# Adding the gate to the normed output on GpSimd, ahead of one output product, in the second retention layer

## The chip, the cores and the metric

One Trainium2 chip, one core. The metric is the device time of one execution in microseconds (us); lower is better. The kernel runs as one launch with one instruction stream for each engine: PE (TensorE, with its weight loads shown as PEld), DVE (VectorE), ACT (ScalarE), POOL (GpSimd) and SP (SyncE, which issues most loads). The engines run their own streams in order and meet only at semaphores.

## What is computed

A two-layer transformer on 16 sequences of 512 tokens, width 128: a retention with a gate, a mixture of eight experts (top two of each token), a second retention, a second mixture of experts, a layer norm behind each. The change lies in the second retention, which is this part of the reference (eight heads of 16):

```
scores = einsum('bnhd,bmhd->bhnm', q, k) * D
ret = einsum('bhnm,bmhd->bnhd', scores, v)
mu, var = mean(ret), var(ret)                     # over the 16 features of a head
ret = (ret - mu) * rsqrt(var + EPS)
ret = ret.reshape(B, S, HIDDEN) * gn_w + gn_b
gated = x @ W1
out = gated * sigmoid(gated) + ret
return out @ W2
```

The residual and the layer norm follow, and then a router: logits of the eight experts, the two largest of them, and the rank that each token gets in its expert's list.

## The kernel before, in words

The second retention is a pipeline over the 16 sequences, written out step by step by hand. In step s the engines work on seven sequences at once, each at another stage. The stages are named by the variables of `turns(s)`: `y` sums the expert results of layer one, `a` (two steps behind the load) makes q, k, v, `b` the scores and the retention itself, `c1` the norm of each head, `c2` the output product, `d` the router, `e` the scatter of rows to the experts. So the output product of a sequence stands one step behind its head norm. The order in each engine's stream is the order of these statements; there is no planner.

What the change touches, in the order of one step:

- PE, `step`: the gate product `x @ W1` (L2384, tile T1) of sequence b, right behind it the eight small matmuls that count the ranks of the router (`ranks_mm_`, L405 to L413) of the sequence that was at d one step earlier, then the scores (L2281). Further on `project_out(c2)`: two rank-one products that put in the constant row (L2312, L2315), and for each of four blocks of 128 tokens the gate's block times `w_2` (L2319) and the normed output's block times `w_2g` (L2321), all summed in the PSUM tile T0. In the profile each product is two instructions. Behind it: the first part of the retention product (L2298), a wait for the second half of the masked scores, the q and k products (L2449, L2450), the transposes of the head norm's factors (L2465).
- ACT: the gate's SiLU into `sgT` (L2021), and `oc`, a copy of the retention's raw output (L2063).
- DVE: `oT` (L2214), the normed output, is `oc` times the transposed factors. Right behind it stands the router's `choose`: copy of the logits, the two largest, their indices, `dif` (L390), a cast (L392), `pick` (L393), `picked` (L398). PE's rank matmuls wait for `picked`. DVE then waits for the ranks and makes the rows (`rows_of`, L421 to L431); behind these stand the masked scores of the first half (L2119), the states, the head norm's inverse root (L209 to L216), the masked scores of the second half, the sums of the expert results (L1640, L1654), the residual `r` (L2129), q and k (L2205, L2206), and `oT` again.
- POOL: four pairs of scatters of sequence e (L477), two small power operations (L295, L297) for the norms of y and c2, then `put_places` of d (a mark at L189, copies at L453 and L456), which waits for a tanh on ACT (L444).
- Set-up on ACT, at the end of layer one: `w_2`, and `w_2g`, which is `w_2` with its rows scaled by `gn_w` (L1093).
- `HELD` (17) is the number of buffers in which layer one's expert results wait for their scatter on POOL (L897); ACT's copy into a buffer (L969) waits until the scatter that last read it has landed.

Of the kernel before, what the change touches and what calls it, by code (L numbers as in the profile page):

```python
# [15 lines left out]
P = 128  # L16
SEQS, T, D = 16, 512, 128
# [87 lines left out]
def build(nc, x, x_T, w_proj, wo, gnorm, rope, router0, gate0, up0, down0,  # L105
# [9 lines left out]
    with whole:  # L115
# [38 lines left out]


        sent_sems = [[whole.enter_context(nc.semaphore(f"sent{l}{i}")) for i in range(2)] for l in range(2)]
        HELD = 17
        st_sems = [[whole.enter_context(nc.semaphore(f"st{l}{i}")) for i in range((HELD, 4)[l])] for l in range(2)]
        used = []

# [460 lines left out]
        def first_layer(block):  # L621
            ph = ExitStack()
            with ph:
# [292 lines left out]
                def _(act):  # L916
# [142 lines left out]
                    for u in range(STEPS + DRAIN):  # L1059
                        unit(u)  # L1060
                        if u == 2:
                            late_rows(t14)
                        if u == 3:
                            late_turned_rows(t14)
                        if u == 4:
                            act.wait_ge(ogT_mm, SEQS)
                            nc.scalar.copy(ogT[:], TT).then_inc(ogT_ev, 1)
                            turned_logits(t14, O)
                            late_copies(t14)
                        if u == 7:  # L1070
                            late_rows(t15)
                        if u == 8:
                            late_turned_rows(t15)
                            late_copies(t15)
                        if u == 9:
                            turned_logits(t15, O)
                        if u == ALONE + 20:
                            exp_piece()
                        if u == ALONE + 24:
                            tanh_piece()  # L1080
                        if u == EARLY_STEPS + 18:
                            comb.norm.squares(act, comb.r[0], first_two[0], comb.used)
                        if u == EARLY_STEPS + 20:
                            comb.norm.squares(act, comb.r[1], first_two[1], comb.used)
                        if u == EARLY_STEPS + 21:
                            comb.norm.apply(act, comb.r[0], xb[0], first_two[0], x2_there)
                        if u == FOLD:
                            act.wait_ge(s_early, 16 * len(early))
                            act.wait_ge(wv_mm, 1)
                            nc.scalar.copy(w_v[:], V_BANK[:, 0:P]).then_inc(wv_there, 1)  # L1090
                            act.wait_ge(w2_mm, 1)
                            nc.scalar.copy(w_2[:], W_BANK[:, 0:P]).then_inc(w2_there, 1)
                            nc.scalar.activation(w_2g[:], W_BANK[:, 0:P], ACT.Copy, scale=g_w[:, 0:1]).then_inc(w2_there, 1)  # L1093
                            comb.norm.apply(act, comb.r[1], xb[1], first_two[1], x2_there)
                        if u == FOLD + 1:
                            act.wait_ge(gb_mm, 1)
                            nc.scalar.copy(gb_hi[:], G_BANK[0:1, 0:D]).then_inc(gb_hi_there, 1)
# [230 lines left out]
                def _(pe):  # L1328
# [215 lines left out]
                    for u in range(STEPS + DRAIN):  # L1544
# [42 lines left out]
                            nc.tensor.matmul(V_BANK[:, 0:P], w_vT[:], c_center[:], start=True, stop=True).then_inc(wv_mm, 1)  # L1587
                            nc.tensor.matmul(W_BANK[:, 0:P], w_2T[:], c_mean[:], start=True, stop=True).then_inc(w2_mm, 1)
                        if u == FOLD + 1:
                            pe.wait_ge(w2_there, 2)  # L1590
                            nc.tensor.matmul(G_BANK[0:1, 0:D], g_b[:], w_2[:], start=True, stop=True).then_inc(gb_mm, 1)

            return Ends(e_y_mm, e_y_there, wv_there, w2_there, set_there)
# [71 lines left out]
        def second_layer(block, first):  # L1665
# [4 lines left out]
            with ph:  # L1670
# [71 lines left out]
                g_mm, sg_there = sem("g_mm"), sem("sg_there")  # L1742
                o_mm, sq_there, oc_there = sem("o_mm"), sem("sq_there"), sem("oc_there")
                var_mm, var_there, ex_mm, oT_there = sem("var_mm"), sem("var_there"), sem("ex_mm"), sem("oT_there")
                yb_there = sem("yb_there")
                y_mm, r_there, x3_there, x3_kept = sem("y_mm"), sem("r_there"), sem("x3_there"), sem("x3_kept")

# [111 lines left out]
                def _(pool):  # L1859
                    norm.set_up(pool)  # L1860

                    def unit(u):
                        n = u - 5
                        if 0 <= n < STEPS:
                            pool.wait_ge(e_idx_there, n + 1)
                            pool.wait_ge(e_y_there, n + 1)
                            for i in range(ROWS // P):
# [2 lines left out]
                                        ap=idx[n % 4][:, i:i + 1], axis=0),  # L1870
                                    in_=ysb[n % 4][:, i, :], in_offset=None).then_inc(e_st[n % 4], 16)

                    def paced(y, a, b, c1, c2, d, e):
                        if e:
                            router.scatter_pair(pool, e, 0)
                            if d:
                                router.scatter_pair(pool, e, 1, router.tp, d.n + 1)
                                router.scatter_pair(pool, e, 2, router.lg_mm, d.n + 1)
                            else:
                                router.scatter_pair(pool, e, 1)  # L1880
                                router.scatter_pair(pool, e, 2)
                            if b:
                                router.scatter_pair(pool, e, 3, sT_there, 4 * b.n + 4)
                            else:
                                router.scatter_pair(pool, e, 3)
                        if y and y.n > 2:
                            comb.norm.power(pool, y)
                        if c2:
                            norm.power(pool, c2)

                    def step(s, fill):
                        _, y, a, b, c1, c2, d, e = turns(s, lags + [7])
# [3 lines left out]
                        else:  # L1896
# [3 lines left out]
                            for q in range(4):  # L1900
                                if e:
                                    router.scatter_pair(pool, e, q)
                            fill(2)
                            fill(3)
                        if d:
# [29 lines left out]
                def _(act):  # L1935
# [58 lines left out]
                    def step(s, fill):  # L1994
# [60 lines left out]
                        if b:  # L2055
# [4 lines left out]
                            wait_count(act, var_mm, b.n)  # L2060
                            nc.scalar.activation(osq[:], O[:, :], ACT.Square).then_inc(sq_there, 1)
                            wait_count(act, oT_there, b.n)
                            nc.scalar.copy(oc[:], O[:, :]).then_inc(oc_there, 1)  # L2063
                        else:
                            fill(3)
                        if d:
# [201 lines left out]
                def _(pe):  # L2268
# [1 line left out]
                    pe.wait_ge(s_cleared, 1)  # L2270
                    pe.wait_ge(first.y_there, STEPS)
                    pe.wait_ge(first.wv_there, 1)
                    pe.wait_ge(first.w2_there, 2)
                    pe.wait_ge(first.set_there, 2)

                    def scores(b, half):
# [30 lines left out]
                                             start=False, stop=False, skip_group_check=True)  # L2307

                    def project_out(c2):
                        pe.wait_ge(oT_there, c2.n + 1)  # L2310
                        pe.wait_ge(sg_there, c2.n + 1)
                        nc.tensor.matmul(T0[:].rearrange("p (c d) -> p c d", c=CH), ones_r[:],  # L2312
                                         gb_hi[:].unsqueeze(1).to_broadcast([1, CH, D]), start=True, stop=False,
                                         skip_group_check=True)
# [1 line left out]
                                         gb_lo[:].unsqueeze(1).to_broadcast([1, CH, D]), start=False, stop=False,  # L2316
                                         skip_group_check=True)
                        for i in range(CH):
                            nc.tensor.matmul(T0[:, i * D:(i + 1) * D], sgT[c2.odd][:, i * P:(i + 1) * P], w_2[:],  # L2319
                                             start=False, stop=False, skip_group_check=True)  # L2320
                            mm = nc.tensor.matmul(T0[:, i * D:(i + 1) * D], oT[:, i * P:(i + 1) * P], w_2g[:],  # L2321
                                                  start=False, stop=True, skip_group_check=True)
                        mm.then_inc(y_mm, 1)

# [170 lines left out]
        with weights:  # L2495
# [12 lines left out]
            def shared_sem(name):  # L2508
                return weights.enter_context(nc.semaphore("b_" + name))

            w_v, w_2, w_2g = (shared_sb(n, [P, P]) for n in ("wv", "w2", "w2g"))
            gb_hi, gb_lo = shared_sb("gb_hi", [1, D], F32R), shared_sb("gb_lo", [1, D], F32R)
            ones_r = shared_sb("ones_r", [1, P], F32R)
            xb = [shared_sb(f"xb{i}", [P, CH, D]) for i in range(2)]
# [93 lines left out]
```

## Time and profile before

| | us |
|---|---|
| median of 3 runs | 1215.84 |
| runs, lowest to highest | 1214.67 to 1220.07 |
| the profiled execution, its own time | 1216.78 |
| span of that execution | 1214.9 |
| second retention, first to last output product in the trace | 570 to 824 |

| engine | busy us | share of the span |
|---|---|---|
| PE | 1119.5 | 92% |
| PEld | 999.6 | 82% |
| DVE | 905.6 | 75% |
| ACT | 742.2 | 61% |
| POOL | 730.4 | 60% |

The shares are means over stages with different limits, and PE's busy time includes matmuls that overlap each other. So the rows further down come from the second retention alone: which engine there waits for which, in the order of time. Two times on DVE can overlap a little, because an instruction is drawn until its last write while the next one has begun.

### The profile page before, as it was taken

To read this page: it belongs to the slowest core of one execution; us is meant where nothing else is said; L and a number is where in the kernel's file an instruction comes from. 1 tells how busy PE (TensorE), PEld (TensorE's weight loads), DVE (VectorE), ACT (ScalarE), POOL (GpSimd) and SP (SyncE) were. 2 spreads that over 40 slices of the span, in tenths; PEclk is the share of its full clock that TensorE was granted. 3 is DMA by queue.
4 is the path that set the end of the run, shared out by engine and by line. 5 is a ranking of instruction groups with operands and counts; after the bars stand their busy time and mean duration, and the time that the engine had idled before them with its cause. 6 is when DMAs were issued, how large, how long until landed. Compare 5 with 4: busy or idle time off the path is not lost.

```text
span 1214.9 us, 31631 instructions
## 1 busy us (share of the span) xinstructions
PE 1119.5 (92%) x10400; PEld 999.6 (82%) x10400; DVE 905.6 (75%) x2648; ACT 742.2 (61%) x2015; POOL 730.4 (60%) x901
## 2 busy tenths in 40 slices
PE   8999999998788999978999999966999999999991
PEld 5888888886678999956777777655899999999991
DVE  4688988998666777747888988865676666667873
ACT  2345435554455777744777888744566666667884
POOL 0257777776467777473366766566744444445765
PEclk9999999999899999989999999977999999999996
DMA  8212111211124433352332211111321121214553
GB/s 235 79 60 73 38 53 48 73 32 55 51 76 128 129 109 108 117 160 69 97 117 67 71 51 49 45 36 45 102 58 55 56 58 56 57 56 123 154 180 123
DMA packets 75423, 101.77 MB, mean 84 GB/s; under 512 B 15138, under 2 KB 51490, under 8 KB 74850
## 3 DMA queue, kind: packets, MB, share of 16 engines
q1 hardware_dynamic: 49538, 59.89, 17.6%
q0 software_dynamic: 17280, 35.69, 8.8%
q10 hardware_dynamic: 8448, 4.20, 1.2%
q8 instruction: 87, 1.43, 0.5%
q14 instruction: 70, 0.57, 0.2%
HBM read 59.87 MB, written 43.04 MB: 85 GB/s over the span
## 4 chain that ended last, share of the span: by engine, by line
PE 69%; DVE 17%; ACT 5%; issue 4%; POOL 2%; SPq 1%; DMA 1%; ACTq 1%; DVEq 0%; POOLq 0%
PE banks L2353 16%; PE banks L2372 10%; PE banks L1444 6%; PE banks L1462 4%; DVE a_sT L1116 3%; PE banks L1353 2%; PE banks L2298 2%; PE banks L1383 2%; PE banks L2290 2%; PE banks L2449 2%; PE banks L2281 2%; ACT a_r_x L260 2%; PE banks L2319 1%; PE banks L1380 1%; DVE a_qm L1218 1%
## 5 line engine op out<-in xcount | busy, mean ns | idle before, releaser
L1868 POOL DMA_INDIRECT expert_out<-e_ysb,b_e_idx x142 | 161.5, 1137 | 149.3 <-ACT e_ysb L1973 122.5
L2353 PE MATMUL banks<-b_e_x_hi,e_w_hi 128*128 128x256 f32 x568 | 166.4, 293 | 4.5 <-ACT e_sgl L1963 2.4
L897 POOL DMA_INDIRECT expert_out<-a_e_ysb,a_e_idx x142 | 140.8, 991 | 44.4 <-issue 36.2
L2353 PE MATMUL banks<-b_e_x_hi,e_w_lo 128*128 128x256 f32 x568 | 159.7, 281 | 0.0
L477 POOL DMA_INDIRECT scattered<-a_r_x,a_r_idx x128 | 127.6, 997 | 33.9 <-issue 33.9
L2372 PE MATMUL banks<-w_dn,e_h 128*128 x1136 | 138.3, 275 | 2.3 <-DVE e_h L2165 1.6
L2372 PEld LDWEIGHTS banks<-w_dn,e_h 128*128 128x128 f32 x1136 | 132.5, 192 | 3.0 <-issue 2.9
L2165 DVE TENSOR_TENSOR e_h<-banks,e_sgl 128x512 f32<-128x512 f32 x142 | 97.1, 689 | 49.5 <-PE banks L2353 47.0
L1963 ACT ACTIVATE e_sgl<-banks 128x512 f32<-128x512 f32 x142 | 85.1, 599 | 74.8 <-DVE e_h L2165 41.8
L477 POOL DMA_INDIRECT scattered<-b_r_x,b_r_idx x112 | 110.0, 982 | 30.9 <-issue 30.9
L2153 DVE TENSOR_TENSOR e_w_lo<-w_gu,e_w_hi 128x1024 fp32r<-128x1024 f32 x71 | 87.0, 1226 | 54.7 <-ACT e_w_hi L1952 54.7
L2353 PEld LDWEIGHTS banks<-b_e_x_hi,e_w_hi 128*128 128x128 f32 x568 | 107.5, 189 | 6.1 <-ACT e_sgl L1963 3.3
L2353 PEld LDWEIGHTS banks<-b_e_x_hi,e_w_lo 128*128 128x128 f32 x568 | 107.2, 189 | 0.0
L2353 PE MATMUL banks<-e_x_lo,e_w_hi 128*128 128x256 f32 x376 | 105.6, 281 | 0.0
L1444 PE MATMUL banks<-a_e_x_hi,a_e_w_hi 128*128 128x256 f32 x284 | 88.4, 311 | 0.2 <-DVE a_e_h L1167 0.2
L2119 DVE TENSOR_TENSOR b_sT<-banks,c_causal 128x1024 f32<-128x1024 f32 x64 | 75.4, 1219 | 15.6 <-PE banks L2281 15.1
L1462 PE MATMUL banks<-w_dn,a_e_h 128*128 x568 | 76.5, 277 | 10.3 <-ACT a_e_ysb L969 10.3
L1952 ACT CAST e_w_hi<-w_gu 128x1024 fp32r x71 | 74.2, 1045 | 13.7 <-PE banks L2353 5.2
L1444 PE MATMUL banks<-a_e_x_hi,a_e_w_lo 128*128 128x256 f32 x284 | 81.9, 288 | 0.0
L1444 PE MATMUL banks<-a_e_x_lo,a_e_w_hi 128*128 128x256 f32 x284 | 81.3, 286 | 0.0
L1462 PEld LDWEIGHTS banks<-w_dn,a_e_h 128*128 128x128 f32 x568 | 69.5, 191 | 13.2 <-issue 13.1
L863 POOL TENSOR_TENSOR a_inv_rms<-a_mse,c_half 128x16 f32<-128x16 f32 x14 | 47.6, 3402 | 45.1 <-DVE a_mse L1133 45.1
(385 smaller groups left out, 3292.1 us busy)
## 6 DMA issues: line engine op xcount, KB each, us to landing
a_e_xg<-scattered SPq DMA_DIRECT2D x71, 130.0 KB
b_e_xg<-scattered SPq DMA_DIRECT2D x71, 130.0 KB, 2.0
b_cy<-expert_out SPq DMA_DIRECT2D x32, 256.0 KB, 3.2
f_y<-expert_out SPq DMA_DIRECT2D x32, 256.0 KB, 3.5
a_xT<-in_x_T SPq DMA_DIRECT2D x16, 256.0 KB, 2.8
out<-f_x ACTq DMA_DIRECT2D x16, 256.0 KB, 2.9
expert_out<-a_e_ysb,a_e_idx POOLq DMA_INDIRECT x142, 2.3
expert_out<-e_ysb,b_e_idx POOLq DMA_INDIRECT x142
```

The costliest lines, as they stand in the source:

```text
L477: nc.gpsimd.indirect_dma_start(out=scattered[0:E * REGION, :], out_offset=bass.IndirectOffsetOnAxis(ap=self.rows_at(t)[:, j:j + 1], axis=0 ...
L897: nc.gpsimd.indirect_dma_start(out=expert_out, out_offset=bass.IndirectOffsetOnAxis(ap=idx[n % HELD][:, i:i + 1], axis=0), in_=ysb[n % HEL ...
L1444: mm = nc.tensor.matmul(bank_of(c)[:, i * ROWS:(i + 1) * ROWS], w_[c % RING][:, g, f:f + P], x_[c % RING][:], start=(k == 0), stop=(k == 2))
L1462: mm = nc.tensor.matmul(y_bank(d)[:, i * D:(i + 1) * D], h[d % RING][:, f, i * P:(i + 1) * P], w_dn[:, bass.ds(e, 1), f, :].rearrange("p o ...
L1868: nc.gpsimd.indirect_dma_start(out=expert_out, out_offset=bass.IndirectOffsetOnAxis(ap=idx[n % 4][:, i:i + 1], axis=0), in_=ysb[n % 4][:, ...
L1952: nc.scalar.copy(w_hi[b % RING][:], w_gu[:, bass.ds(e, 1), :, :].rearrange("p o g f -> p (o g) f")).then_inc(e_w_hi_there, 1)
L1963: nc.scalar.activation(sgl[j][:], gate_bank(c, j)[:].rearrange("p (k n) -> p k n", k=2), ACT.Silu).then_inc(e_sg_there, 1)
L2119: nc.vector.tensor_tensor(sT[half][:, 2 * g:2 * g + 2, :, :].rearrange("p g n t -> p (g n) t"), pairs[2 + g].rearrange("p g (n t) -> p (g ...
L2153: nc.vector.tensor_tensor(w_lo[b % RING][:], w_gu[:, bass.ds(e, 1), :, :].rearrange("p o g f -> p (o g) f"), w_hi[b % RING][:].bitcast(F32 ...
L2165: nc.vector.tensor_tensor(h[c % RING][:, 2 * j:2 * j + 2, :], up_bank(c, j)[:].rearrange("p (k n) -> p k n", k=2), sgl[j][:], ALU.mult).th ...
L2353: mm = nc.tensor.matmul(bank_of(c, j)[:, i * ROWS:(i + 1) * ROWS], w_[c % RING][:, g, f:f + P], x_[c % RING][:], start=(m == 0), stop=(m = ...
L2372: mm = nc.tensor.matmul(y_bank(d)[:, i * D:(i + 1) * D], h[d % RING][:, f, i * P:(i + 1) * P], w_dn[:, bass.ds(e, 1), f, :].rearrange("p o ...
```

## The change

The gate and the normed output are added before the output product, so that `w_2` is applied once and not twice. For that the norm's weight `gn_w` moves from `w_2g` into ACT's copy `oc`, which becomes an activation with a scale for each partition; `w_2g` and the ACT instruction that made it are gone. The sum is one POOL instruction, `oT = oT + sgT` (128 by 512, f32), with its own semaphore `osum_there`; PE's `project_out` waits for that one in place of `oT_there` and `sg_there`. For that semaphore one of layer one's result buffers is given up (`HELD` 17 to 16). The rank matmuls keep their place behind the gate product.

```
-        HELD = 17
+        HELD = 16
...
-                            nc.scalar.activation(w_2g[:], W_BANK[:, 0:P], ACT.Copy, scale=g_w[:, 0:1]).then_inc(w2_there, 1)
...
+                    def gated_sum(c1):
+                        pool.wait_ge(oT_there, c1.n + 1)
+                        pool.wait_ge(sg_there, c1.n + 1)
+                        nc.gpsimd.tensor_tensor(oT[:], oT[:], sgT[c1.odd][:], ALU.add).then_inc(osum_there, 1)
...
                         if c2:
                             norm.power(pool, c2)
+                        if c1:
+                            gated_sum(c1)
...
                             for q in range(4):
                                 if e:
                                     router.scatter_pair(pool, e, q)
+                            if c1:
+                                gated_sum(c1)
...
-                            nc.scalar.copy(oc[:], O[:, :]).then_inc(oc_there, 1)
+                            nc.scalar.activation(oc[:], O[:, :], ACT.Copy, scale=g_w[:, 0:1]).then_inc(oc_there, 1)
...
                     def project_out(c2):
-                        pe.wait_ge(oT_there, c2.n + 1)
-                        pe.wait_ge(sg_there, c2.n + 1)
+                        pe.wait_ge(osum_there, c2.n + 1)
...
                         for i in range(CH):
-                            nc.tensor.matmul(T0[:, i * D:(i + 1) * D], sgT[c2.odd][:, i * P:(i + 1) * P], w_2[:],
-                                             start=False, stop=False, skip_group_check=True)
-                            mm = nc.tensor.matmul(T0[:, i * D:(i + 1) * D], oT[:, i * P:(i + 1) * P], w_2g[:],
+                            mm = nc.tensor.matmul(T0[:, i * D:(i + 1) * D], oT[:, i * P:(i + 1) * P], w_2[:],
                                                   start=False, stop=True, skip_group_check=True)
```

POOL in one step of the full pipeline, before: the last pair of scatters, the two power operations of the norms, and the places.

```order
L477 DMA scattered<-b_r_x,b_r_idx 67584x130 x2
L295 TENSOR_TENSOR b_cn_ve<-b_cn_var,b_cn_eps 128x4
L297 TENSOR_TENSOR b_cn_rstd<-b_cn_ve,c_half 128x4
L295 TENSOR_TENSOR b_n_ve<-b_n_var,b_n_eps 128x4
L297 TENSOR_TENSOR b_n_rstd<-b_n_ve,c_half 128x4
L189 TENSOR_TENSOR mark<-c_half 1x1
L453 COPY b_r_x<-c_place 128x4
```

The same piece of POOL's stream after the change:

```order
L477 DMA scattered<-b_r_x,b_r_idx 67584x130 x2
L295 TENSOR_TENSOR b_cn_ve<-b_cn_var,b_cn_eps 128x4
L297 TENSOR_TENSOR b_cn_rstd<-b_cn_ve,c_half 128x4
L295 TENSOR_TENSOR b_n_ve<-b_n_var,b_n_eps 128x4
L297 TENSOR_TENSOR b_n_rstd<-b_n_ve,c_half 128x4
L1876 TENSOR_TENSOR b_oT<-b_oT,b_sgT 128x512
L189 TENSOR_TENSOR mark<-c_half 1x1
L453 COPY b_r_x<-c_place 128x4
```

One instruction came in, between the last power operation and the places of the same step.

POOL in the last but two steps of the pipeline (s = 19), after the change, where the step has another order: the norm's power operations, the scatters of a sequence in one go, and the sum behind them.

```order
L295 TENSOR_TENSOR b_n_ve<-b_n_var,b_n_eps 128x4
L297 TENSOR_TENSOR b_n_rstd<-b_n_ve,c_half 128x4
L189 TENSOR_TENSOR mark<-c_half 1x1
L477 DMA scattered<-b_r_x,b_r_idx 67584x130 x8
L1876 TENSOR_TENSOR b_oT<-b_oT,b_sgT 128x512
```

Here the last sequence's sum stands behind eight scatters; before, no instruction of POOL stood between the last sequence's `oT` and its output product.

PE in one step, from the router's logits to the q and k products, before (the pair L2319, L2321 stands there four times):

```order
L364 MATMUL banks<-b_wr,b_r_xT 128x8 x4
L2312 MATMUL banks<-b_gb_hi,b_ones_r 128x512
L2315 MATMUL banks<-b_gb_lo,b_ones_r 128x512
L2319 MATMUL banks<-b_w,b_sgT 128x128
L2321 MATMUL banks<-b_w2g,b_oT 128x128
...
L2298 MATMUL banks<-b_sT,b_vz 32x128 x8
L2449 MATMUL banks<-b_xT,b_wq 128x512
```

And after (the lines have moved by six to nine):

```order
L364 MATMUL banks<-b_wr,b_r_xT 128x8 x4
L2320 MATMUL banks<-b_gb_hi,b_ones_r 128x512
L2323 MATMUL banks<-b_gb_lo,b_ones_r 128x512
L2327 MATMUL banks<-b_w,b_oT 128x128 x4
L2307 MATMUL banks<-b_sT,b_vz 32x128 x8
L2455 MATMUL banks<-b_xT,b_wq 128x512
```

Four of the eight products are gone from each of the 16 output products; nothing else in PE's stream moved.

## Rows read from the trace of the kernel before

**Rows 1.** Busy us by engine in a stretch; columns: PE, PEld, DVE, ACT, POOL, PEclk, DMA.

```profile
570.00:760.00 190.00, 188.06 (x2043) 145.30 (x2043) 168.08 (x598) 145.25 (x497) 118.43 (x212) 1.00 0.24 73
```

**Rows 2.** Waits in 560 to 800: us in total, times, longest.

```profile
DVE b_r_rows L421 <- PE banks L413: 9.0, 12, 0.8
```

**Rows 3.** Timeline of DVE in one step: start us, us, operation [idle before].

```profile
689.90 2.35 DVE L2119 TENSOR_TENSOR b_sT<-banks,c_causal 128x1024 f32<-128x1024 f32 x2
...
695.12 0.68 DVE L2205 TENSOR_TENSOR b_qr<-banks,b_tq 128x512 f32<-128x512 f32 x1
695.72 0.68 DVE L2206 TENSOR_TENSOR b_kT<-banks,b_tk 128x512 f32<-128x512 f32 x1
696.49 0.69 DVE L2214 TENSOR_TENSOR b_oT<-banks,b_oc 128x512 f32<-128x512 f32 x1
...
698.69 0.23 DVE L393 TENSOR_TENSOR b_r_pick<-c_iota,b_r_ix 128x64 f32<-128x64 f32 x1
698.95 0.19 DVE L398 TENSOR_TENSOR b_r_picked<-b_r_pick 128x32 bf16<-128x32 f32 x1
...
699.91 0.19 DVE L421 TENSOR_TENSOR b_r_rows<-banks,base 128x32 f32<-128x32 f32 x1 [0.77 <-PE banks L413]
```

**Rows 4.** Timeline of PE in the same step, to the next step's q product.

```profile
692.63 1.12 PE L2449 MATMUL banks<-b_xT,b_wq 128*128 128x512 f32 x2
...
699.53 0.18 PE L405 MATMUL banks<-b_r_picked,c_tri 128*128 128x32 bf16 x1
...
707.67 0.39 PE L2319 MATMUL banks<-b_w,b_sgT 128*128 128x128 f32 x2
707.90 0.39 PE L2321 MATMUL banks<-b_w2g,b_oT 128*128 128x128 f32 x2
...
709.68 1.12 PE L2449 MATMUL banks<-b_xT,b_wq 128*128 128x512 f32 x2
```

**Rows 5.** Timeline of POOL in the same step.

```profile
697.45 1.01 POOL L297 TENSOR_TENSOR b_n_rstd<-b_n_ve,c_half 128x4 f32<-128x4 f32 x1
700.57 0.18 POOL L189 TENSOR_TENSOR mark<-c_half 1x1 f32<-1x1 f32 x1 [2.11 <-ACT b_r_th L444]
```

**Rows 6.** Timeline of DVE and PE at the ranks of step 17.

```profile
786.93 0.19 DVE L398 TENSOR_TENSOR b_r_picked<-b_r_pick 128x32 bf16<-128x32 f32 x1
...
787.17 0.19 PE L405 MATMUL banks<-b_r_picked,c_tri 128*128 128x32 bf16 x1 [0.83 <-DVE b_r_picked L398]
...
787.57 0.19 DVE L421 TENSOR_TENSOR b_r_rows<-banks,base 128x32 f32<-128x32 f32 x1 [0.45 <-PE banks L413]
```

**Rows 7.** Timeline of PE and POOL at the last sequence's output product.

```profile
819.53 0.79 PE L2312 MATMUL banks<-b_gb_hi,b_ones_r 1*128 1x512 f32 x1
...
820.81 0.96 POOL L477 DMA_INDIRECT scattered<-b_r_x,b_r_idx  x1 [0.30 <-issue]
```

**Rows 8.** Busy us by engine there; columns as in rows 1.

```profile
820.00:824.00 4.00, 4.00 (x17) 3.35 (x17) 0.61 (x5) 0.00 (x0) 2.23 (x7) 0.50 0.10 33
```

**Rows 9.** Timeline of DVE and POOL, two places where both read SBUF.

```profile
706.22 0.24 DVE L214 TENSOR_TENSOR b_gn_sq<-b_gn_y 128x32 f32<-128x32 f32 x1
706.24 0.96 POOL L477 DMA_INDIRECT scattered<-b_r_x,b_r_idx  x1 [0.30 <-issue]
...
810.40 1.23 DVE L2153 TENSOR_TENSOR e_w_lo<-w_gu,e_w_hi 128x1024 fp32r<-128x1024 f32 x1 [1.92 <-ACT e_w_hi L1952]
810.66 1.01 POOL L189 TENSOR_TENSOR mark<-c_half 1x1 f32<-1x1 f32 x1
```

**Rows 10.** POOL's groups by line: busy us, mean ns of one.

```profile
L841 POOL MEMSET c_half<- 128x64 f32 x1 | 0.2, 151 | 0.3 <-POOLq L2598 0.3
L844 POOL MEMSET a_wr<- 128x24 f32 x1 | 0.1, 118 | 0.0
```

**Rows 11.** Timeline of ACT at the set-up of the second retention.

```profile
520.74 0.37 ACT L1093 ACTIVATE b_w2g<-banks,b_gw 128x128 f32<-128x128 f32 x1
521.00 1.27 ACT L303 ACTIVATE b_xb<-b_cr,b_cn_rstd 128x128 f32<-128x128 f32 x4
```

More of the change, by code:

```diff
@@ L1589, in _ @@
                         if u == FOLD + 1:
-                            pe.wait_ge(w2_there, 2)
+                            pe.wait_ge(w2_there, 1)
                             nc.tensor.matmul(G_BANK[0:1, 0:D], g_b[:], w_2[:], start=True, stop=True).then_inc(gb_mm, 1)
@@ L1744, in second_layer @@
                 var_mm, var_there, ex_mm, oT_there = sem("var_mm"), sem("var_there"), sem("ex_mm"), sem("oT_there")
+                osum_there = sem("osum_there")
                 yb_there = sem("yb_there")
@@ L2272, in _ @@
                     pe.wait_ge(first.wv_there, 1)
-                    pe.wait_ge(first.w2_there, 2)
+                    pe.wait_ge(first.w2_there, 1)
                     pe.wait_ge(first.set_there, 2)
@@ L2509, in shared_sem @@
                 return weights.enter_context(nc.semaphore("b_" + name))
-            w_v, w_2, w_2g = (shared_sb(n, [P, P]) for n in ("wv", "w2", "w2g"))
+            w_v, w_2 = (shared_sb(n, [P, P]) for n in ("wv", "w2"))
             gb_hi, gb_lo = shared_sb("gb_hi", [1, D], F32R), shared_sb("gb_lo", [1, D], F32R)
```

## The prediction

> **What bounds the kernel now.** The mean shares say PE (92%), so I read the stage that is changed by itself: first busy time by stage, then the waits, then one step on three engines in the order of time. In the full pipeline PE is busy 188 of 190 us at its full 2.4 GHz level (granted clock 1.00), but DVE is busy 168 of them too [rows 1], and the small gaps between dependent DVE instructions come on top. A step takes 17.05 us (709.68 less 692.63) [rows 4]. Of DVE's idle time one wait stands out: 12 times, 9.0 us in all, it waits for the router's ranks [rows 2]. One step shows why [rows 3, 4]. `picked` ends at 699.14 (698.95 + 0.19). The rank matmul starts at 699.53, 0.39 later, with no idle time shown before it: PE was still in the gate product that stands ahead of it. DVE goes on at 699.91. In step 17, where PE had nothing else to do, `picked` ends at 787.12, the matmul starts 0.05 later, and DVE goes on 0.45 after `picked` [rows 6], not 0.77. So PE and DVE are both nearly full and hold each other at the ranks. A shorter PE stream alone is worth what DVE can follow, no more.
>
> **The change part by part.**
>
> Four products fewer. Products follow each other 0.23 us apart (707.67, 707.90) [rows 4]; the eight take some 1.8 us, so four save 0.9 us in each step, 14 us of PE in 16. What lies behind them decides what is kept. The q product L2449 may start only when DVE has ended the second half of the masked scores: 689.90 + 2.35 = 692.25, and it started at 692.63 [rows 3, 4]. With the reaction time of 0.05 to 0.06 [rows 6] it can start at 692.31, so PE keeps 0.32 of the 0.9; the rest becomes a wait for the mask. The gate product and the ranks follow 0.32 earlier, at 699.21. DVE can deliver: `oT` stood 0.77 behind `kT`, while `kT` stood 0.60 behind `qr` [rows 3]; I read the 0.17 as a wait for PE's transposes, which goes, and `picked` then ends at 698.97, ahead of 699.21. So without any other effect a full step gets 0.32 us shorter.
>
> The sum on POOL. No row shows such an instruction. Two fills on POOL give a slope: 33 ns for 40 elements [rows 10], 0.8 ns an element, about 0.1 us to begin with. The write alone, 512 elements, is 0.5 us; two reads in turn and a write beside them 0.95; all three in turn 1.4. I take 1.2 us, between the last two, and keep 0.5 and 1.4 as ends. In place it costs POOL nothing: the power operation ahead of it ends at 698.46, and the mark behind it starts at 700.57, after 2.11 us of idle time [rows 5]. `oT` is there at 697.18, so the sum runs from 698.46 to about 699.66. The places are not late until it takes more than 2.1 us, and PE's output product comes some 8 us later in the next step.
>
> What it costs is DVE. Just then DVE has `pick` and `picked` to do, each with both inputs in SBUF, and PE's ranks wait for them. Two rows show that POOL and DVE do not read freely side by side [rows 9]. POOL's mark, one element, lasts 1.01 us where a mark takes 0.18 [rows 5]: it ends at 811.67, when DVE's subtraction of two SBUF tiles (810.40 to 811.63) ends. POOL is held for all of DVE's instruction. The other way round the trace has only short cases: a DVE product of two SBUF inputs takes 0.24 where the same line elsewhere takes 0.19, as POOL's scatter starts 0.02 behind it and fetches its indices. So the hold on DVE lies between 0.05 us and the whole sum. I take the whole: the full hold is what the long case shows, and the sum, unlike the scatter, reads from its beginning to its end. `pick` would start at 698.52 (698.69 less 0.17) and has to wait until 699.66; from its start to the end of `picked` it is 0.45 (698.69 to 699.14), so 700.11; 0.45 more for the ranks gives 700.56, where DVE now goes on at 699.91. That is 0.65 us more in a step: the hold of 1.14 less the waits of 0.49 that the shorter PE stream has opened. By the ends of the sum (0.95 and 1.4) it is 0.40 and 0.85.
>
> The Trainium skill has a rule for this (SBUF — State Buffer, Who interferes with whom): a DVE instruction with two SBUF inputs and a GpSimd instruction that reads SBUF share one read interface, whichever starts first has it for the whole instruction, and the other "fully blocks". The first case of rows 9 agrees (1.01 us); no run here shows the reverse at length. By that rule a step is 0.65 longer, by the short row alone (0.05) it is 0.27 shorter. The same skill (GPSIMD Engine Reference, Performance versus the Vector engine) gives 4497 ns for an add of 2048 columns; a quarter, as an estimate, is 1.1 us, and a step would then be 0.55 longer; no row here shows it.
>
> How many steps. The wait for ranks stands in 12 steps, 6 to 17 [rows 2]; I charge each 0.65: 7.8 us. In the four steps ahead of them no ranks are counted, and the sum meets no DVE work that matters: nothing.
>
> The last two output products. There the step has another order and the clock is at the 1.2 GHz level (0.50) [rows 8], so four products are worth 1.8 us (twice 0.9). The last but one gives that, and pulls forward all behind it, POOL's eight scatters too. The last one loses it again: its sum stands behind these scatters, which end at 821.77 (820.81 + 0.96), 2.24 later than PE starts now [rows 7]. With 1.8 earlier scatters: 819.97 + 1.2 = 821.2, that is 1.6 late, against 1.8 saved by its own four products. Net I take 0; between 1 gained and 1 lost.
>
> The small parts. `w_2g` frees 0.26 us of ACT (521.00 less 520.74) [rows 11], back to back with what starts the second retention: 0.26 gained, between 0 and that. `oc` with a scale instead of a copy is the same kind of ACT instruction with the same tile, off the path: 0. One buffer fewer (`HELD`): the trace lists no wait of ACT for a free buffer; a wait would cost a pair of scatters, 2 x 1.26 us as in rows 7 (0.96 + 0.30), once or twice. I take 0.
>
> Sum: 7.8 - 0.26 + 0 = 7.5 us. The profiled execution took 1216.78, so 1224.3; it lies 0.94 above the median of the runs, so the median comes to 1215.84 + 7.5 = 1223.3.
>
> **The rivals.**
>
> *DVE is not held, or hardly.* Then the shorter PE stream counts: 12 x 0.32 = 3.8, 0.26 from ACT, and 0 to 1 at the end, together 4.6: 1211.2 (with all ends 1209.5 to 1212). For it: the only rows with DVE second show 0.05 us; against it: the full hold on POOL. It decides at a hold of 0.49 us in a step: below, the change gains.
>
> *The sum takes far longer than the fills suggest*, 2 us, because its reads wait for DVE's in between. Then a step is 1.45 longer, 12 x 1.45 = 17.4: 1233. For it: POOL waited 0.8 us for one DVE instruction [rows 9]; against it: behind `pick` and `picked` DVE has only short ones.
>
> *The clock falls.* PE would idle about 2 us in each step of 17.7; if the granted clock then fell to its 1.2 GHz level now and then, as it is in rows 8 after long waits, the 16 us of PE work would outgrow the step: one such stretch of 4 us costs up to 2 us of PE, hidden by the idle time at first. Several in each step would give over 1235. Against it: the idle time is cut into pieces of 1 us.
>
> *The change does not do what it says*: the four products are gone in the order of instructions, so only the price of each could be wrong; that is in the first rival.
>
> **How the numbers follow.** DVE held for about the sum: 0.64, own range 1219.5 (0.40 a step, and 1 gained at the end) to 1227 (0.85, and 1 lost). Not held: 0.25. A far longer sum: 0.08. Clock: 0.03. Faster by over 0.5% (about what a measurement of this kernel can tell from no change; 6.1 us, so below 1209.8) needs the first rival at its end: 0.07. Slower by over 0.5% (above 1221.9) is most of the held case, 0.45, and the last two: 0.56. The rest, 0.37, is within. The range reaches down to the first rival and up past the held case: 1210 to 1228.
>
> **What would show it.** In the profile after: a POOL instruction of 128x512 right behind `b_n_rstd`, about 1.2 us; `pick` on DVE starting at its end, where it now follows the cast at once; PE idle before the rank matmul, about 1 us, for `picked`; steps of 17.7 us. If `pick` starts on time and steps are 16.7 us, the hold was wrong. If steps are longer but `pick` is on time, look for what else is late. In the last step, the output product should start right behind the sum, not behind the ranks.

## The result, and the profile after

The changed kernel takes 1224.82 us in the median of 9 runs (1222.37 to 1227.9), the kernel before 1215.84: ratio 1.0068, 95% interval 1.0056 to 1.0080. It is slower by about 9 us; the forecast was 1223.3. The profiled execution of after took 1222.74 (span 1220.9), that of before 1216.78, so the two traces account for 6.0 us; the other 3 lie between executions that were not traced, and stay open. One execution of before_sum (2664.55) and one of held16 (2716.24) took more than twice as long as the others, and the medians further down leave them out.

Three rows of one full step carry the result. First POOL, in the order of time (start us, us, operation, idle before):

```profile
698.13 1.01 POOL L297 TENSOR_TENSOR b_n_rstd<-b_n_ve,c_half 128x4 f32<-128x4 f32 x1
699.11 1.26 POOL L1876 TENSOR_TENSOR b_oT<-b_oT,b_sgT 128x512 f32<-128x512 f32 x1
701.01 0.18 POOL L189 TENSOR_TENSOR mark<-c_half 1x1 f32<-1x1 f32 x1 [0.64 <-ACT b_r_th L444]
```

The sum takes 1.26 us and stands where POOL was idle: the mark still waits 0.64 for ACT, where it waited 2.11 [rows 5]. Now DVE in the same step:

```profile
697.00 0.68 DVE L2223 TENSOR_TENSOR b_oT<-banks,b_oc 128x512 f32<-128x512 f32 x1
...
698.91 0.17 DVE L390 TENSOR_TENSOR b_r_dif<-b_r_mx 128x4 f32<-128x4 f32 x1
...
699.20 1.25 DVE L393 TENSOR_TENSOR b_r_pick<-c_iota,b_r_ix 128x64 f32<-128x64 f32 x1
700.49 0.19 DVE L398 TENSOR_TENSOR b_r_picked<-b_r_pick 128x32 bf16<-128x32 f32 x1
...
701.13 0.19 DVE L421 TENSOR_TENSOR b_r_rows<-banks,base 128x32 f32<-128x32 f32 x1 [0.45 <-PE banks L413]
```

`pick` lasts 1.25 us where it lasted 0.23 [rows 3]. It is not shown as waiting: it is drawn from 699.20 on and ends (700.45) just behind the sum (700.37). The ranks are then 0.45 away, as in step 17 of before [rows 6], not 0.77. And PE:

```profile
692.99 1.12 PE L2455 MATMUL banks<-b_xT,b_wq 128*128 128x512 f32 x2 [0.31 <-DVE b_sT L2128]
...
699.02 1.02 PE L2390 MATMUL banks<-b_xT,b_w 128*128 128x512 f32 x2
700.74 0.19 PE L405 MATMUL banks<-b_r_picked,c_tri 128*128 128x32 bf16 x1 [0.69 <-DVE b_r_picked L398]
...
710.30 1.12 PE L2455 MATMUL banks<-b_xT,b_wq 128*128 128x512 f32 x2 [0.25 <-DVE b_sT L2128]
```

PE now waits twice in a step for DVE: 0.69 for `picked`, and 0.25 to 0.31 for the masked scores. The step is 17.31 us (710.30 less 692.99), where it was 17.05 [rows 4]. Over 190 us PE is busy 177.73, DVE 173.13, and the granted clock stays at 1.00, the 2.4 GHz level; the row of before is in [rows 1]:

```profile
570.00:760.00 190.00, 177.73 (x1933) 132.04 (x1931) 173.13 (x593) 142.70 (x488) 132.01 (x221) 1.00 0.23 72
```

### The profile page after: what moved, and what is told of

Its sections match the earlier page's. It is cut to its first block, busy times and chain, and to the rows that moved or that the text cites. A ratio compares the mean times of both kernels' runs of the same rounds, so it can differ in the third digit from the quotient of the medians.

```text
span 1220.9 us, 31402 instructions
## 1 busy us (share of the span) xinstructions
PE 1111.4 (91%) x10272; PEld 987.3 (81%) x10272; DVE 915.7 (75%) x2648; ACT 741.8 (61%) x2014; POOL 749.2 (61%) x917
## 3 DMA queue, kind: packets, MB, share of 16 engines
q8 instruction: 86, 1.41, 0.5%
## 4 chain that ended last, share of the span: by engine, by line
PE 57%; DVE 26%; issue 6%; ACT 5%; POOL 3%; SPq 1%; DMA 1%; ACTq 1%; DVEq 0%; POOLq 0%
PE banks L2359 16%; PE banks L2378 10%; PE banks L1443 6%; PE banks L1461 4%; DVE a_sT L1115 3%; DVE b_sT L2128 3%; PE banks L1382 2%; PE banks L1352 2%; PE banks L2299 2%; ACT a_r_x L260 1%; PE banks L1379 1%; DVE a_qm L1217 1%; PE banks L356 1%; DVE b_r_pick L393 1%; PE banks L2343 1%
```

## Where the time went, for all kernels

Four stretches add up to the span of a profile. Head: to the q product of step 6 (590.36 in before). Eleven steps: from there to the q product of step 17. Drain: to the start of the last residual `r`. Rest: the second mixture of experts and the end. The step in brackets is the mean of the eleven; in no_sum and late_last, for instance, one step that is longer than the others lifts it by up to 0.1. The lower rows are the experiments that follow; each ratio there is to runs of the kernel before taken beside it (medians 1215.56 to 1216.14).

| kernel | median us | head | eleven steps (one) | drain | rest |
|---|---|---|---|---|---|
| before | 1215.84 | 590.36 | 187.49 (17.04) | 46.65 | 390.40 |
| after | 1224.82 | 588.84 | 190.68 (17.33) | 49.71 | 391.67 |
| no_sum | 1208.62 | 588.47 | 182.04 (16.55) | 45.10 | 390.79 |
| before_sum | 1230.15 | 590.78 | 194.13 (17.65) | 52.97 | 390.72 |
| sum_early | 1212.45 | 589.64 | 181.85 (16.53) | 48.94 | 390.67 |
| sum_halves | 1224.14 | 591.32 | 189.21 (17.20) | 50.64 | 391.43 |
| last_dve | 1221.21 | 589.93 | 190.51 (17.32) | 46.71 | 391.45 |
| early_last | 1211.54 | 591.38 | 182.16 (16.56) | 45.99 | 390.67 |
| sum_late | 1215.51 | 589.19 | 181.14 (16.47) | 48.90 | 391.37 |
| sum_dve | 1217.66 | 591.12 | 187.57 (17.05) | 47.61 | 391.30 |
| late_last | 1209.77 | 589.72 | 182.20 (16.56) | 44.58 | 390.50 |
| held16 | 1216.85 | 591.27 | 187.51 (17.05) | 46.58 | 390.24 |

Between before and after the stretches differ by -1.52, +3.19, +3.06 and +1.27, together +6.0. The head varies by 2.9 us among kernels that hardly differ there, so its -1.52 is no gain that can be claimed; the rest varies by 1.4, so neither is its +1.27 a loss. The eleven steps and the drain are where the change acts, and each loses about 3 us.

The drain of after, PE, POOL and DVE in the order of time:

```profile
788.35 0.97 DVE L390 TENSOR_TENSOR b_r_dif<-b_r_mx 128x4 f32<-128x4 f32 x1
...
805.17 1.19 DVE L390 TENSOR_TENSOR b_r_dif<-b_r_mx 128x4 f32<-128x4 f32 x1
...
807.27 0.49 PE L2320 MATMUL banks<-b_gb_hi,b_ones_r 1*128 1x512 f32 x1
...
810.11 0.69 DVE L2138 TENSOR_TENSOR b_r<-banks,xres 128x512 f32<-128x512 f32 x1 [1.67 <-PE banks L2327]
...
823.61 0.96 POOL L477 DMA_INDIRECT scattered<-b_r_x,b_r_idx  x1 [0.30 <-issue]
824.59 1.27 POOL L1876 TENSOR_TENSOR b_oT<-b_oT,b_sgT 128x512 f32<-128x512 f32 x1
...
826.00 0.76 PE L2320 MATMUL banks<-b_gb_hi,b_ones_r 1*128 1x512 f32 x1 [3.62 <-POOL b_oT L1876]
...
829.23 0.69 DVE L2138 TENSOR_TENSOR b_r<-banks,xres 128x512 f32<-128x512 f32 x1 [5.75 <-PE banks L2327]
```

And of before, beside [rows 7]:

```profile
803.49 0.49 PE L2312 MATMUL banks<-b_gb_hi,b_ones_r 1*128 1x512 f32 x1
...
807.32 0.69 DVE L2129 TENSOR_TENSOR b_r<-banks,xres 128x512 f32<-128x512 f32 x1 [2.68 <-PE banks L2321]
...
824.50 0.69 DVE L2129 TENSOR_TENSOR b_r<-banks,xres 128x512 f32<-128x512 f32 x1 [3.81 <-PE banks L2321]
```

In the last two steps the held instruction is `dif` (0.97 and 1.19 for 0.17). The last but one product takes 2.84 us to its residual, 3.83 before. From that residual to the last product it is now 15.89, before 12.21: eight scatters and the sum stand ahead of it. The last product then takes 3.23, before 4.97. With 2.11 until the last but one product (27.75 for 25.64) that is 2.11 - 0.99 + 3.68 - 1.74 = 3.06.

## Experiments

The theory: the sum holds a DVE instruction with two SBUF inputs until it ends, and in the drain the last sum stands behind the scatters. All kernels start from the changed one unless the text says otherwise.

**no_sum**, the four products fewer alone; the gate is missing from the output.

```diff
-                        if c1:
-                            gated_sum(c1)
...
-                            if c1:
-                                gated_sum(c1)
...
-                        pe.wait_ge(osum_there, c2.n + 1)
+                        pe.wait_ge(oT_there, c2.n + 1)
+                        pe.wait_ge(sg_there, c2.n + 1)
```

> The changed kernel with the POOL sum taken out; PE's output product waits for the normed output and the gate directly and multiplies the normed output alone, four products, so the gate is missing from the output. It shows what the four products fewer are worth without the sum. Theory of the hold (the sum keeps DVE's pick waiting 1.03 us a step): pick is back at 0.22 us, the step falls from 17.33 to between 16.45 and 16.75, the last output product no longer waits behind the scatters, and the time is 1203 to 1210. Rival (DVE is the bound with or without the sum, so four products less on PE bring nothing): the step only goes back to the 17.05 of the kernel before, the time is 1213 to 1217.

Measured: 1208.62, ratio to before 0.9944 (0.9926 to 0.9962); the full steps are 16.50.

```profile
694.21 0.23 DVE L393 TENSOR_TENSOR b_r_pick<-c_iota,b_r_ix 128x64 f32<-128x64 f32 x1
...
695.27 0.19 DVE L421 TENSOR_TENSOR b_r_rows<-banks,base 128x32 f32<-128x32 f32 x1 [0.61 <-PE banks L413]
```

`pick` is back at 0.23. So four products fewer are worth 0.5 us in a step and 7 us in all, the last output products included; the rival falls. The wait for ranks is 0.61 here, not 0.45: without the hold PE's gate product is again the later of the two.

**before_sum**, the sum alone, beside the eight products.

```diff
+                        nc.gpsimd.tensor_tensor(scratch[:], oT[:], sgT[c1.odd][:], ALU.add).then_inc(osum_there, 1)
...
-                        pe.wait_ge(oT_there, c2.n + 1)
-                        pe.wait_ge(sg_there, c2.n + 1)
+                        pe.wait_ge(osum_there, c2.n + 1)
```

> The kernel before with its eight products, and the POOL sum beside them into a tile that nobody reads; the output product waits for it as in the changed kernel (one result buffer is given up for the semaphore). It shows the sum's price by itself. Theory of the hold: pick takes 1.25 us instead of 0.22, the rank matmuls start 0.69 later than before (1.03 less the 0.39 that PE was still busy, and 0.05 of reaction), the step is 17.45 to 17.75, and with the last product behind scatters and sum (3.5 later) the time is 1225 to 1231. Rival (the sum costs DVE nothing that the pipeline feels; the loss of the changed kernel is in its last steps alone): the step stays at 17.05, the time is 1217 to 1221.

Measured: 1230.15, ratio 1.0118 (1.0096 to 1.0141), step 17.65. Time and step lie in the band; the held instruction was another. One step, POOL and DVE:

```profile
702.20 1.26 POOL L1878 TENSOR_TENSOR b_scratch<-b_oT,b_sgT 128x512 f32<-128x512 f32 x1
...
702.43 1.06 DVE L390 TENSOR_TENSOR b_r_dif<-b_r_mx 128x4 f32<-128x4 f32 x1
703.41 0.16 DVE L392 CAST b_r_ix<-b_r_mi 128x8 f32<-128x8 uint32 x1
703.60 0.23 DVE L393 TENSOR_TENSOR b_r_pick<-c_iota,b_r_ix 128x64 f32<-128x64 f32 x1
```

Here the sum starts 0.23 us ahead of `dif`, and `dif`, four columns long, pays: it lasts until 703.49, the sum until 703.46. In these runs the first instruction with two SBUF inputs that comes behind the sum's start is the one that is held, however short it is. That the step came so near is in part luck: the hold of 0.89 less the 0.32 at the ranks gives 0.57 of the 0.60, but two more terms that nobody had forecast cancel (`oT` stands 1.02 behind `kT` for 0.77, and the two masked scores stand 5.71 apart for 5.93).

**sum_halves**, two POOL instructions of 256 columns.

```diff
-                        nc.gpsimd.tensor_tensor(oT[:], oT[:], sgT[c1.odd][:], ALU.add).then_inc(osum_there, 1)
+                        for h in range(2):
+                            op = nc.gpsimd.tensor_tensor(oT[:, 256 * h:256 * h + 256], oT[:, 256 * h:256 * h + 256],
+                                                         sgT[c1.odd][:, 256 * h:256 * h + 256], ALU.add)
+                        op.then_inc(osum_there, 1)
```

> The changed kernel with the sum as two POOL instructions of 256 columns each. Theory that one instruction has the read port until its end and then lets the other engine in: pick is held by the first half alone and takes 0.6 to 0.75 us, the step is 16.7 to 16.95, the time 1216 to 1220. Rival that POOL keeps it as long as it has work queued: pick takes 1.25 us or more, step and time stay (17.3, 1224).

Measured: 1224.14, ratio 1.0066 (1.0044 to 1.0088), step 17.20.

```profile
700.70 1.41 POOL L1877 TENSOR_TENSOR b_oT<-b_oT,b_sgT 128x256 f32<-128x256 f32 x2
700.78 0.72 DVE L393 TENSOR_TENSOR b_r_pick<-c_iota,b_r_ix 128x64 f32<-128x64 f32 x1
701.53 0.62 DVE L398 TENSOR_TENSOR b_r_picked<-b_r_pick 128x32 bf16<-128x32 f32 x1
```

`pick` takes 0.72, as the theory of one lock for each instruction says; but then the second half holds `picked` (0.62 for 0.19). What this expectation left out is that `picked` also reads two SBUF operands. Together the hold is 0.92 in place of 1.03, and step and time miss the band: they lie near the rival's 17.3 and 1224, though the 0.72 of `pick` is not the rival's 1.25. Here the split gave the time between the two halves to the next reader, which the second half then held.

**sum_early**, the sum ahead of the second power operation, beside DVE instructions with at most one SBUF input.

```diff
-                        if c2:
-                            norm.power(pool, c2)
                         if c1:
                             gated_sum(c1)
+                        if c2:
+                            norm.power(pool, c2)
```

> The changed kernel with the sum moved on POOL ahead of the second power operation, so that it runs while DVE copies the logits (from PSUM) and takes maxima and indices (one SBUF input each), and is over when pick comes. Theory that the sum holds only an instruction with two SBUF inputs: pick is back at 0.22 us, the maxima and indices keep their times, the step is 16.45 to 16.75, the time is 1207 to 1214 (the last product still stands behind the scatters). Rival that the sum holds every DVE instruction that reads SBUF: some of the maxima or the copy become about 1 us longer, the step stays at 17.3, the time at 1223 to 1226.

Measured: 1212.45, ratio 0.9968 (0.9951 to 0.9984), steps of 16.50.

```profile
693.82 0.17 DVE L378 MAX8 b_r_mx<-b_r_lg 128x8 f32<-128x8 f32 x1
...
693.87 1.27 POOL L1876 TENSOR_TENSOR b_oT<-b_oT,b_sgT 128x512 f32<-128x512 f32 x1
693.90 0.29 DVE L378 MAX8 b_r_mx<-b_r_lg 128x8 f32<-128x8 f32 x3
...
694.91 0.26 DVE L390 TENSOR_TENSOR b_r_dif<-b_r_mx 128x4 f32<-128x4 f32 x1
...
695.36 0.23 DVE L393 TENSOR_TENSOR b_r_pick<-c_iota,b_r_ix 128x64 f32<-128x64 f32 x1
695.38 1.09 POOL L297 TENSOR_TENSOR b_n_rstd<-b_n_ve,c_half 128x4 f32<-128x4 f32 x1
695.62 0.19 DVE L398 TENSOR_TENSOR b_r_picked<-b_r_pick 128x32 bf16<-128x32 f32 x1
```

The same sum, of the same length, costs the step nothing here (16.50, as in no_sum): the maxima keep their times, and only `dif`, which starts 0.23 us before the sum ends, lasts 0.09 longer. The rival that the sum holds any read of SBUF falls. By moving one statement the change becomes faster than the kernel before.

**sum_late**, the sum behind the places, beside the masked scores.

```diff
-                        if c1:
-                            gated_sum(c1)
...
                             router.put_places(pool, d)
+                        if c1 and (y or a or b):
+                            gated_sum(c1)
```

> The changed kernel with the sum moved on POOL behind the places of its step, so that it runs beside DVE's masked scores (one input in PSUM, one in SBUF); the scatters of the next step come 1.2 us later, into POOL's idle time ahead of the places. Theory that only an instruction with two SBUF inputs is held: the masked scores keep their 2.35 us, pick its 0.22, the step is 16.45 to 16.75 and the time 1209 to 1215. Rival that one SBUF input is enough if the instruction reads it all along: the masked scores take about 3.5 us, the step is 17.3, the time 1222 to 1226.

Measured: 1215.51, ratio 0.9996 (0.9986 to 1.0005); the profiled execution, at 1212.49, is the lowest of its ten runs.

```profile
696.37 2.36 DVE L2128 TENSOR_TENSOR b_sT<-banks,c_causal 128x1024 f32<-128x1024 f32 x2
...
696.78 1.27 POOL L1876 TENSOR_TENSOR b_oT<-b_oT,b_sgT 128x512 f32<-128x512 f32 x1
```

The masked scores, one input in PSUM and one in SBUF, keep their 2.36 us with the sum inside them, and the step is 16.47: the theory holds. The median lies 0.5 us above the band, and 3 us above the profiled run; what differs in the other runs was not traced and stays open.

**last_dve**, the last sequence's sum on DVE.

```diff
-                            if c1:
-                                gated_sum(c1)
...
+                            if not (y or a or b):
+                                dve.wait_ge(oT_there, c1.n + 1)
+                                dve.wait_ge(sg_there, c1.n + 1)
+                                nc.vector.tensor_tensor(oT[:], oT[:], sgT[c1.odd][:], ALU.add).then_inc(osum_there, 1)
```

> The changed kernel with the last sequence's sum on DVE, right behind its normed output, and the other 15 on POOL as before. It tests the last output product. In the changed kernel it starts at 826.00, behind eight scatters and the sum, 3.6 us after the ranks. Theory (this wait is on the path to the end): DVE's sum takes about 0.65 (estimate: half of the 1.23 of its 1024-column subtraction of two SBUF tiles), the ranks come that much later and the product right behind them at about 822.9, so the time falls by 3.1, to 1220 to 1223. Rival (the experts that follow wait for something else): the product is earlier, the time stays at 1224 to 1225.

Measured: 1221.21, ratio 1.0041 (1.0027 to 1.0056).

```profile
820.87 0.69 DVE L2225 TENSOR_TENSOR b_oT<-b_oT,b_sgT 128x512 f32<-128x512 f32 x1
...
823.89 0.79 PE L2322 MATMUL banks<-b_gb_hi,b_ones_r 1*128 1x512 f32 x1
```

The last product starts right behind the ranks, and the drain is 46.71, that of before (46.65), for 49.71. So the wait behind the scatters is worth 3.0 us and is on the path to the end.

**early_last**, both at once.

> Both at once: the sum ahead of the second power operation, and the last sequence's sum on DVE. If the hold and the last product are separate costs, the time is that of the early sum (1212.5) less 3.1: 1207.5 to 1211, below the kernel before. If the last product was hidden, it is 1211 to 1214.

Measured: 1211.54, ratio 0.9963 (0.9947 to 0.9978), half a microsecond above the band and inside that of its rival (1211 to 1214), so the median alone does not decide. In the traces the two gains add: 16.56 a step and a drain of 45.99 for 48.94. The median shows 0.9 of these 3 us: the runs spread over 5 us, and the profiled execution's head is 1.7 longer than that of sum_early.

**sum_dve**, all sums on DVE.

> The changed kernel with all 16 sums on DVE, right behind the normed output, and none on POOL. Theory (DVE is the bound of the step once PE has four products less): each sum adds its own 0.6 to 0.7 us to a step of 16.50, so the step is 17.1 to 17.2 and the time 1215 to 1220, less than the changed kernel's because nothing is held and the last product does not wait for scatters. Rival (DVE, busy 75% of the span, has room): the step stays at 16.5, the time at 1208 to 1211.

Measured: 1217.66, ratio 1.0011 (0.9999 to 1.0023), step 17.05.

```profile
698.12 0.69 DVE L2218 TENSOR_TENSOR b_oT<-b_oT,b_sgT 128x512 f32<-128x512 f32 x1
...
698.28 0.59 POOL L295 TENSOR_TENSOR b_n_ve<-b_n_var,b_n_eps 128x4 f32<-128x4 f32 x1
```

The step lies just under the band (17.1 to 17.2). The sum takes 0.69 on DVE, and a step grows by 0.5 over no_sum; the wait for the ranks, 0.45 here for 0.61 there, gives back 0.16. So DVE has no more room than that, though it is busy only 75% of the span. The second row is the hold in the other direction: POOL's operation of four columns takes 0.59 for 0.19, until DVE's sum ends. So the sum takes less of DVE's time when DVE makes it (0.69) than when POOL makes it beside `pick` and holds DVE (1.03).

**late_last**, the late place in full steps, the early one in the last full step, the last sum on DVE. What the expectation calls the second to the thirteenth q product is the stretch from the fourth (573.07 in sum_late) to the sixteenth (770.33).

> The sum behind the places while the pipeline is full, ahead of the second power operation in the last full step (where the late place made the output product wait 2.09 us for it), and on DVE for the last sequence. By the parts of the traces so far: 197.3 us from the second to the thirteenth q product as with the late sum, then 46.0 to the last residual as with the early sum and the last on DVE, which is 7.6 less than before (250.85): 1207 to 1210. Rival (the late sum's runs scattered from 1212.5 to 1218 because its later scatters cost something that its one profile does not show): 1212 to 1216.

Measured: 1209.77, ratio 0.9954 (0.9937 to 0.9971): the lowest median of a complete kernel here, though early_last's interval (0.9947 to 0.9978) overlaps. The mean step is 16.56 and the drain 44.58, the shortest of all. By the medians it is about 15 us faster than the changed kernel with the same work. The median speaks for the theory, but three of the 12 runs lie above 1212 (up to 1217.21): the spread of the runs that the rival pointed at is still there, and its cause stays open.

**held16**, the kernel before with one result buffer fewer.

> The kernel before with 16 result buffers in the first layer in place of 17 and nothing else. Theory that no copy ever waits for the seventeenth buffer: ratio 1.000, 1214.5 to 1217. Rival that a copy waits once or twice for a pair of scatters (2.5 us each): 1218 to 1221.

Measured: 1216.85, ratio 1.0007 (0.9995 to 1.0019). No cost shows; the interval leaves room for at most 2.3 us, less than one such wait.

## Why the prediction was right, and where its steps were off

The sum's length and its place: 1.2 us was taken, 1.26 measured. The two halves give 0.71 each (1.41 for two), so it goes by 2.2 ns a column and 0.15 to begin with, between two and three times the fills' 0.8 ns an element. The prediction had bounded it so (0.95 to 1.4) and picked 1.2 without a row that says where between: there it was lucky.

The hold: 1.14 was charged, 1.03 measured (1.25 less 0.22), and no_sum, sum_early and sum_late show that it is the cause: without the sum, or with it beside instructions with other operands, the step is 16.5. One sign came otherwise: `pick` does not start at the sum's end, it starts on time and lasts. The rule of the Trainium skill that the prediction set beside [rows 9] (SBUF — State Buffer, Who interferes with whom) agrees for the sum in both directions: DVE instructions with two SBUF inputs are held until it ends (1.06 for `dif`), POOL's are held by DVE's sum (0.59 for 0.19). Beside the sum, one SBUF input is not held (`MAX8` at 0.17, masked scores at 2.36); beside a scatter that is not so, as the next rows show.

The step: 0.65 longer was forecast, 0.26 to 0.29 came. The step of the sum that failed is "the hold less the waits of 0.49 that the shorter PE stream has opened". The 0.49 was there (0.32 at the ranks, 0.18 from `r` to `oT`: 1.80 for 1.98), but 0.27 more was: between the two masked scores 5.66 us now (702.23 to 707.89), 5.93 before. The place is the inverse root. Groups of DVE over all 16 sequences (busy us, mean ns), before:

```profile
L210 DVE TENSOR_SCALAR b_gn_bits<-b_var 128x32 int32<-128x32 int32 x16 | 4.6, 290 | 0.0
L209 DVE TENSOR_SCALAR b_gn_half<-b_var 128x32 f32<-128x32 f32 x16 | 4.5, 283 | 0.5
```

and after:

```profile
L209 DVE TENSOR_SCALAR b_gn_half<-b_var 128x32 f32<-128x32 f32 x16 | 3.2, 202 | 0.5
L210 DVE TENSOR_SCALAR b_gn_bits<-b_var 128x32 int32<-128x32 int32 x16 | 2.9, 180 | 0.0
```

Both read one SBUF input. In each of the eleven steps of before, L210 ends together with one of POOL's scatters, in seven of them L209 too. One such place of before, POOL and DVE:

```profile
703.63 0.96 POOL L477 DMA_INDIRECT scattered<-b_r_x,b_r_idx  x1 [0.30 <-issue]
...
704.13 0.43 DVE L209 TENSOR_SCALAR b_gn_half<-b_var 128x32 f32<-128x32 f32 x1
704.23 0.36 DVE L210 TENSOR_SCALAR b_gn_bits<-b_var 128x32 int32<-128x32 int32 x1
```

All three end at 704.56 to 704.59. After the change the two start just ahead of a scatter or at its very beginning, and mostly take 0.18 each. In no_sum they lie inside a scatter, but earlier in it, and are not held either:

```profile
633.09 0.96 POOL L477 DMA_INDIRECT scattered<-b_r_x,b_r_idx  x1 [0.30 <-issue]
...
633.47 0.18 DVE L209 TENSOR_SCALAR b_gn_half<-b_var 128x32 f32<-128x32 f32 x1
633.56 0.17 DVE L210 TENSOR_SCALAR b_gn_bits<-b_var 128x32 int32<-128x32 int32 x1
```

The traces of all twelve kernels agree: from 560 to 830 us, where one of these two starts up to 0.49 us into a scatter, it takes 0.17 to 0.21; where it starts 0.53 or more into it, it ends no earlier than 0.03 us before the scatter does (at 0.50 and 0.51 both occur). So the kernel before already lost 0.27 in each step, and the new phase of the scatters took that away: 1.03 - 0.32 - 0.18 - 0.27 = 0.26. Of the 0.27, 0.19 stands at these two (from `b_var` to the next instruction 0.52 us for 0.71) and 0.05 at the square at 706.22, where another scatter begins [rows 9]. No experiment moved the scatters alone, so that they are the cause rests on this agreement. The same missing term made the first rival too small: it allowed 0.32 a step for four products, no_sum shows 0.5. By these terms the change gains from a hold under 0.77, not 0.49; sum_halves fits, with a hold of 0.92 and a step 0.15 longer than before.

The drain: 0.65 was forecast (the last of the twelve charged steps, and net 0 for the products), +3.06 came. Two terms were off. The last but one product gave 0.99, not 1.8: TensorE's clock was not at the lower level from its start. In before it was granted 0.99 from 804.10 to 804.90, the 2.4 GHz level, and 0.50 from 805 to 807, the 1.2 GHz level; after, it was 0.50 from 808.00 on, so nearly all of the four products that are left ran at the lower level. (PE had waited 1.73 us for `picked` ahead of it in before, 2.76 after.) And the hold of the last two steps, on `dif` (0.80 and 1.02), was charged once and at 0.65. The late start of the last product, behind the scatters, came as worked out (15.7 after the residual forecast, 15.89 measured), and last_dve priced it.

So the eleven steps (7.15 forecast, 3.19 measured: 4.0 too much) and the drain (2.4 too little) cancelled in part, and the head and the rest, which the change hardly touches, moved by more than the 0.26 of `w_2g` could show. The total was right by its cause; that it came so near is in part luck, for the sizes of its parts were off and made up for each other, and 3 of the 9 us between the medians lie in no trace. The clock rival had nothing: 1.00 in the full pipeline. The rival of a far longer sum had nothing either.

## What to carry to other kernels

Before work is moved to an idle engine, look at what its neighbour is reading at that moment: the idle time on POOL was real, and still the sum cost DVE 1.03 us a step, while 1.4 us earlier (sum_early) or 2.7 later (sum_late), counted from `pick`, it cost the step nothing. A held instruction shows as a long one, not as a wait, so compare the mean of one line between two profiles. And where a pipeline drains in another order than it runs, place the new step there by itself: here that alone was 3 us.

## What the runs showed of the hardware that I had not expected

POOL and DVE do not meet only at semaphores, as the part ahead of the prediction has it: they also hold each other while they read SBUF, and no wait shows it. But a POOL instruction does not hold DVE merely by being long. In sum_early the power operation (1.09 us, four columns) runs from 695.38 on, and `picked`, with two SBUF inputs, starts inside it at 695.62 and takes its usual 0.19. The sum, which reads 512 columns, holds to its end. A scatter holds the two inverse-root instructions, each with one SBUF input, in its second half and not in its first. And a DVE instruction of four columns can last 1.2 us (`dif` at 805.17) when it comes behind such a sum.
